# SyncE's list of transfers in a two-layer transformer kernel: the maxima's transfer moves to the head of each slot, and the cross attentions' stack transfers go out one slot later, over six slots

## What is computed

```python
def _attn(q, k, v, mask):
    s = jnp.einsum('bqhd,bkhd->bhqk', q, k) * scale
    s = jnp.where(mask, s, jnp.finfo(s.dtype).min)
    a = jax.nn.softmax(s, axis=-1)
    return jnp.einsum('bhqk,bkhd->bqhd', a, v)
x = x + g_msa * (_attn(q, k, v, attn_mask)            @ attn_out_W)   # layer 1, self
x = x + g_x   * (_attn(qc, kc, vc, cond_kv_mask)      @ co_W)         # layer 1, cross
x = x + g_mlp * (gelu(xm @ mlp_W1 + mlp_b1) @ mlp_W2 + mlp_b2)
x = x + (softmax(q k^T / sqrt(8)) v) @ Wp + bp                        # layer 2, cross
```

## Time and profile before

| | |
|---|---|
| three runs | 1225.09, 1233.65, 1235.43 us; median 1233.65 |
| the profiled execution | 1229.72 us, of which 1227.9 us are the span from first to last instruction |
| mean granted TensorE clock | 0.951 |
| self attention | about 23.9 us per group of 8 slots |
| cross attentions | about 17.5 us per group of 8 slots |

### The profile page before, as it was taken

How to read it: one execution, slowest core, us unless ns; L and a number is a source line. 1 busy time by engine, 2 the same in 40 slices (tenths; PEclk the granted TensorE clock), 3 DMA queues, 4 the chain that set the end, 5 groups by cost and what they waited for, 6 DMA issues and landing times.

```text
span 1227.9 us, 42336 instructions
## 1 busy us (share of the span) xinstructions
PE 1077.5 (88%) x16226; PEld 616.0 (50%) x16226; DVE 827.2 (67%) x2195; ACT 849.3 (69%) x1527; POOL 854.1 (70%) x1804
## 2 busy tenths in 40 slices
PE   5768988898889888989988898999998999999987
PEld 4435444444444445545554563444444565665655
DVE  4347777787876877878888774222325887887875
ACT  2236566656665668878888768878885887876765
POOL 2467767767777767877887634667887887787741
PEclk9779999999998999989999869999998999998998
DMA  6755555655555456666766640000304676777661
GB/s 164 174 105 99 99 99 96 110 98 91 96 95 101 84 78 104 102 100 102 113 103 102 105 65 3 1 1 1 54 14 72 108 126 116 123 118 121 110 114 32
DMA packets 165018, 110.40 MB, mean 90 GB/s; under 512 B 42553, under 2 KB 164434, under 8 KB 164818
## 3 DMA queue, kind: packets, MB, share of 16 engines
q1 hardware_dynamic: 161744, 105.97, 51.1%
q10 hardware_dynamic: 3074, 1.72, 0.5%
HBM read 9.71 MB, written 4.19 MB: 11 GB/s over the span
## 4 chain that ended last, share of the span: by engine, by line
PE 37%; POOL 20%; issue 11%; ACT 11%; SPq 8%; DMA 7%; DVE 4%; ACTq 1%; POOLq 0%; DVEq 0%
SPq L1004 7%; DMA stacks<-mt 7%; PE ps_po L535 6%; ACT p L812 5%; PE ps_st L514 4%; PE ps_st L547 4%; PE ps_pj L416 4%; PE ps_po L556 4%; POOL whole L907 3%; PE ps_nat L486 3%; POOL parts L908 3%; PE ps_pj L411 3%; PE ps_pj L433 3%; POOL ht L939 2%; PE ps_pj L424 2%
## 5 line engine op out<-in xcount | busy, mean ns | idle before, releaser
L619 DVE TENSOR_REDUCE negmax<-ps_nat 128x8 f32<-128x616 f32 (+1 forms) x384 | 360.0, 937 | 71.7 <-PE ps_nat L486 61.3
L812 ACT ACTIVATE p<-ps_st 128x1024 f32<-128x1024 f32 (+1 forms) x256 | 261.1, 1020 | 204.1 <-PE ps_st L514 203.3
L535 PE MATMUL ps_po<-p,vz 77*32 77x128 f32 (+1 forms) x6144 | 259.3, 289 | 3.4 <-ACT p L812 2.1
L514 PE MATMUL ps_st<-stacks 64*77 64x128 bf16 (+1 forms) x3072 | 158.9, 224 | 40.0 <-DMA stacks<-mt 29.7
L812 ACT ACTIVATE p<-ps_st,key_bias 77x1024 f32<-77x1024 f32 x128 | 141.9, 1109 | 50.6 <-PE ps_st L514 49.4
L535 PEld LDWEIGHTS ps_po<-p,vz 77*32 77x32 f32 (+1 forms) x6144 | 151.4, 112 | 43.3 <-issue 7.4
L896 POOL TENSOR_TENSOR ot<-vv,den 128x128 f32<-128x128 f32 x192 | 87.7, 457 | 116.8 <-ACT den L800 109.9
L486 PEld LDWEIGHTS ps_nat<-stacks 64*128 64x128 bf16 x3072 | 79.3, 97 | 137.5 <-issue 124.1
L486 PE MATMUL ps_nat<-stacks 64*128 64x77 bf16 (+1 forms) x3072 | 135.6, 210 | 9.9 <-DVE negmax L619 7.4
L907 POOL TENSOR_TENSOR whole<-whole,parts 128x512 f32<-128x512 f32 x96 | 98.8, 1029 | 61.3 <-ACT parts L747 61.2
L514 PEld LDWEIGHTS ps_st<-stacks 64*77 64x77 bf16 (+1 forms) x3072 | 108.4, 111 | 54.4 <-ACT p L812 28.8
(11 more groups left out here) (149 smaller groups left out, 2141.7 us busy)
## 6 DMA issues: line engine op xcount, KB each, us to landing
stacks<-parts SPq DMA_DIRECT2D x512, 128.0 KB, 3.2
stacks<-parts SPq DMA_DIRECT2D x256, 77.0 KB, 2.8
stacks<-mt SPq DMA_DIRECT2D x192, 32.0 KB, 2.8
p<-in_x_dram SPq DMA_DIRECT2D x16, 256.0 KB
out_dram<-part SPq DMA_DIRECT2D x16, 256.0 KB, 2.3
ot<-in_ctx_dram SPq DMA_DIRECT2D x8, 154.0 KB
gated<-in_ctx_dram SPq DMA_DIRECT2D x8, 154.0 KB
stacks<-in_L_xcond_adaLN_W_dram SPq DMA_DIRECT2D x1, 576.0 KB, 4.2
```

The costliest lines, as they stand in the source:

```text
L514: m = t.matmul(c.ps_st[h][0:nk, S * g:S * g + S], kst[half(h), par, at, nk * j:nk * j + nk], qst[half(h), par, at, S * j:S * j + S], start ...
L535: m = t.matmul(c.ps_po[step % 2][32 * g:32 * g + 32, S * p:S * p + S], c.vz[0:nk, i % 2, step % G, g, at:at + 32], c.p[0:nk, hh, S * g:S * ...
L619: v.tensor_reduce(c.negmax[:, step % 2, :].rearrange("p (h q g) -> p h q g", h=2, q=2)[:, :, p, :], c.nat_pair[:].rearrange("p (h n) -> p ...
L812: a.activation(c.p[0:nk, 2 * p:2 * p + 2, :].rearrange("p h n -> p (h n)"), c.st_pair[0:nk, :], ACT.Exp, bias=bias).then_inc(exped, 1)
```

## The change

Only the order of SP's list changes. In every slot the maxima's transfer is issued ahead of the slot's stacks. In the cross attentions (`starts[1]`) the stacks' slots change as well; no transfer is added, removed or resized, and no wait is changed.

```diff
@@ -1009,7 +1009,7 @@
             starts = {0: ((6, 0, (0, 1, 2)), (7, 0, (3, 4, 5)), (8, 0, (6, 7)), (9, 1, (0, 1, 2)), (10, 1, (3, 4, 5)), (11, 1, (6, 7))),
-                      1: ((7, 0, (0, 1, 2)), (8, 0, (3,)), (8, 1, (0, 1)), (9, 1, (2, 3)), (9, 0, (4,)), (10, 0, (5, 6, 7)), (11, 1, (4, 5, 6)), (12, 1, (7,)))}
+                      1: ((8, 0, (0, 1, 2)), (9, 0, (3,)), (9, 1, (0,)), (10, 1, (1, 2, 3)), (11, 0, (4, 5)), (12, 0, (6, 7)), (12, 1, (4,)), (13, 1, (5, 6, 7)))}
@@ -1033,10 +1033,10 @@
+                if even(unit_at(slot + 3)):
+                    bring_max(unit_at(slot + 3) // 2)
                 for i, x, t in at_slot.get(slot, []):
                     bring_stack(i, x, t)
-                if even(unit_at(slot + 3)):
-                    bring_max(unit_at(slot + 3) // 2)
```

## The result

The changed kernel is slower: median 1292.43 us (1280.32 to 1298.44) against 1233.16 us for the kernel before in the same runs, ratio 1.047 with a 95% interval of 1.041 to 1.053. The profiled execution has a span of 1285.0 us, 57.1 us more than before.

A forecast was written before the change was run, and what follows sets the result against it. It took the cross attentions to hang on SP's issuing, PE waiting 29.7 us for late maxima. From the 1233.65 us median, + 19.2 - 6.4 - 10.8 = + 2, less something for the outer waits, gave 1234 us; eight-in-ten range 1220 to 1248.

The forecast's parts named there:

- All 40 waits for the maxima: Cross attentions: PE's waits before `transposed` for the maxima's DMA, 29.7 us in all, would all go.
- `natural` of +15 waits for k7 instead: Cross attentions, slot +15: a new PE wait about once per group, 0.5 to 1 us each, 20 to 28 us in all.
- the interval from the copy of +13: Cross attentions, end of that copy to `natural` of +15: 5.0 us (4.8 to 5.6) against 4.20 before.
- M+13 itself is late: Rival, cross attentions: that maxima transfer leaves up to 0.4 us late, interval 5.6 us, 1251 us; chance 0.14.
- + 13 (19.2 - 6.4): Cross attentions: 24 groups 0.8 us longer each cost 19.2 us; four long groups save 6.4 us.
- the 24 groups called undisturbed: Both cross attentions before the change: interval from +13 copy to `natural` of +15 said to run 3.97 to 4.65, mean 4.20 us.
- a landing 0.5 us shorter: k7's landing at the skill's 2.2 us, not 2.7: interval 4.5 us, whole some 9 us less, 1225; outside the sum.
- the waits at +10 and +12: Cross attentions: 18 PE waits for the maxima outside the interval, removed for a gain of 10.8 us (8 to 14).
- k7 is covered: Rival, slot +15: k7 lands before anything else frees `natural`, interval 3.97 us, 25 to 28 us gained, about 1207; chance 0.10.
- The order does not matter: Rival: landings are late from the stacks' bytes, not SP's issues; waits at +14 stay, time stays 1234 us; chance 0.06.

The follow-up runs named there:

- experiment 5: Changed kernel with only q6, q7 and k4 between the maxima transfers of +11 and +13, k5 to k7 still behind the latter: 1250.32 us, ratio 1.019 to the kernel before.
- experiments 3 and 4: Changed kernel with k5 to k7 issued ahead of M+13: 1259.68 us, ratio 1.019; with k5 and k6 ahead, k7 alone behind: 1284.08 us, ratio 1.041.
- experiment 6: Changed kernel plus eight matmuls per group on PE at the end of slot +14, result unread: 1258.8 us, ratio 1.025 to the kernel before.
- experiments 1, 2 and 7: Kernel before with maxima first, old slots: 0.987; with new slots, maxima last: 0.985; changed kernel with q7 and k4 to k7 all ahead of M+13: 0.988.

## Why the prediction was wrong

**Right.** All 40 waits for the maxima went; `natural` of +15 waits for k7 instead, once per group (but 69.6 us in all and not 20 to 28); the interval from the copy of +13 is the term on which the sum hangs; the self attention, prologue and MLP hardly move. In experiment 5, where that chain acts without a backlog, the interval is 5.27 us, inside the 4.8 to 5.6 of the forecast and above its 5.0.

**The term that was mis-sized: the interval of 5.0 us.** It measured 6.02. M+13 leaves 0.80 us behind its copy and not 0.03; three issues take 2.22 us and not 1.95; k7's landing takes 2.91 and not 2.7; 0.1 more until PE goes. The forecast took a value near the fastest pitch, 0.65, though its own rows of six had 0.72 to 0.78: over the five tiles between two maxima that is the difference between SP being on time and falling behind. That was written down as a rival, "M+13 itself is late", with 0.14, an interval up to 5.6 and 1251 us. Its sign came true, k7's issue over 2.5 us behind the copy (3.02), so it should have been the forecast; but its size was too small as well, since it let M+13 be 0.4 us late at most. The count that gives the 3.02 is the one under experiments 3 and 4: nine issues from M+11 to k7, 6.8 us, against 4.2 us between the copies. In sum the interval cost + 40 us where the forecast had + 13 (19.2 - 6.4). On two smaller points: the 24 groups called undisturbed have the mean of 4.20, but run from 3.28 to 5.19 us and not from 3.97 to 4.65; and a landing 0.5 us shorter is by the forecast's own sum worth 12 us, not 9. By the Trainium skill, DMA: Bandwidth & Descriptors, Anatomy of one DMA, k7 would by estimate have landed in 2.2 us; with 2.91 measured, its correction pointed the wrong way.

**The term that was missing: the clock.** For the rest I had - 10.8 us, the waits at +10 and +12. That part was nearly right: PE's idle time there fell by 15.0 us. But PE's busy time rose by 28.3, and the rest came out at + 13.3. With the clock held up (experiment 6) it was - 14.7. So 28 us, half of the loss, is clock. Nothing in the forecast asked what PE's standing in one piece does, though the rows had signs of it: L514 took 0.65 us at 544.34 behind a wait of 2.15, and L486 0.44 us at 687.88. The Trainium skill has it in TensorE: Matmul & The Clock Gate, section HAM oscillation — how this bites in real kernels: in a matmul kernel that waits 3 to 5 us for a DMA in every tile, the clock goes down each time, so that each tile starts slow. The trace agrees in part: behind 1.93 and 2.57 us of standing L486 takes 0.45 us and not 0.31, but only 21 of the 28 groups lost clock, most of them behind shorter waits than that.

**The rivals.** "k7 is covered": no. "The order does not matter", with the Trainium skill's sentence in DMA: Bandwidth & Descriptors, Issuing engines are not separate DMA queues, that issuing is usually small relative to the DMA: one issue is indeed the smaller part here, 0.60 us (median) against 2.91 to land, but there are twenty of them per group of 17.7 us. Three orders of the same 20 transfers are 1214 to 1218 us, two others 1284 and 1292.

**Of the change itself:** either half alone makes the kernel 1.3 to 1.5% faster. Together they put the last three tiles behind the copy of +13 and five more between M+11 and M+13, nine issues where the copies leave time for five. The kernels of experiments 1, 2 and 7 are faster than the kernel before and the changed one.

## What to carry to other kernels

Count a queue's list as a serial resource: number of issues up to the one that somebody waits for, times the mean pitch of issues back to back (not the fastest), against the time between the points to which it is tied; whoever moves many short waits to one place must check the last item of the list. And look at how a wait is cut: with 40 waits of 0.7 us PE spent 58 us of the 28 groups at 1.2 GHz, with waits of 2.3 us in one piece 140 us, and that cost 28 us more on top of the 40 us in the intervals.

## What the hardware showed that was not expected

- With one wait of 2.3 us on average in each group of some 20 us, PE's granted clock fell below 1.00 in 21 of 28 groups: in group 27 to a mean of 0.83, at 1.2 GHz from about the end of the wait on, for the next slots. Eight useless matmuls inside the wait left 6 such groups and took the kernel from 4.7% to 2.5% over the one before.
- Some 6 to 9% of SP's DMA issues in the cross attentions take over 1 us against a median of 0.60, so the mean pitch is 0.73 to 0.77 us whatever the order; with two issues per group from ScalarE's queue it rose to 0.84.
